# Attention scores as bf16 products over 72 rows of exact three-part splits, brought from device memory, with masks on the outer thirds and keys folded in 32-column products

## The chip, the cores and the metric

The kernel runs on one core of a Trainium2 chip. The metric is the device time of one execution in microseconds, median of the runs shown; lower is better.

## What is computed

Sliding-window attention without projections over 4096 tokens of 128 features (16 heads of 8), then a post-norm feed-forward layer, then a product-key expert layer. The part that the change touches most:

```python
H = 16; W = 32                       # heads, block of queries; keys: own block and a block on each side
kc = kp[:, :, idx, :]                # 96 keys for every 32 queries
scores = jnp.einsum('bhcqd,bhckd->bhcqk', qc, kc)
valid = (jnp.abs(rel) <= w) & (k_pos >= 0) & (k_pos < S)
scores = jnp.where(valid[None, None], scores, -1e9)
p = jax.nn.softmax(scores, axis=-1)
out = jnp.einsum('bhcqk,bhckd->bhcqd', p, vc)
```

In the expert layer, queries `x @ w_q` are normalised over all tokens and compared with keys. The kernel folds normalisation and keys into one matrix, `w_sim`, and a row of constants, `c_rows`.

## The kernel before, in words

The program has three long stages: attention (32 tiles of 128 tokens), layer norms and feed-forward (8 groups of 512 tokens), and the expert layer (32 tiles). Each engine has its own instruction list, written out by hand, and semaphores join them. In `over_pairs` a loop body is written for the first step, looped, and written for the last; in the attention stage a step is a pair of tiles.

At the start, TensorE transposes all of x into `xT` in fp32, and ScalarE copies it out of PSUM. For a tile t of the attention stage, in two halves of 8 heads each:

- GpSimd makes `queries` (the tile of `xT` times a 0/1 column for each head of a group, L457) and copies v into `v_ones` (L462); VectorE makes `windows` (`group_windows`, L1026): keys masked by group. With these zeros a product over all 128 rows gives one head's scores.
- TensorE's `scores` puts the mask into PSUM with a bf16 product over all 384 columns of a bank (L635), and adds 32 fp32 products of 96 columns (L640). Each half has two PSUM banks of its own, free again once `shift` has read them.
- VectorE's `shift` takes the row maximum (L999) and subtracts it (L1002); ScalarE's `exps` follows (L864); TensorE transposes the probabilities (L653); ScalarE copies them (L848); TensorE's `values` multiplies with v (L666); VectorE's `normalise` scales (L1011, L1015); TensorE's `attn_out` brings heads into columns (L677); VectorE's `residual` adds x from `x_tile` (L1021).

All DMAs are issued by SyncE (SP), in order. In the attention loop it loads `v_raw` for a tile when the v of two tiles before has been copied, then `x_tile` when the residual of two tiles before is done:

```python
need(sp, r1_done, t - 1)
sp.dma_start(x_tile[p][:], x[tok(t), :]).then_inc(x_in[p], 16)
```

`r1_done` counts residuals, so `x_load` of tile t waits for the residual of tile t-2. VectorE runs the residual of tile t-1 in its step t, behind a shift of tile t+1. The weights are loaded behind the first pair's loads.

After the second stage, `q_moments` to `scale_keys` on VectorE and the products L777 (constants) and L781 (16 keys, weights of 128 columns) on TensorE make `c_rows` and `w_sim`; the first similarity product (L791) of the expert stage waits for both.

## Time and profile before

| | us |
|---|---|
| median of 3 runs | 789.24 (786.45 to 789.26) |
| profiled execution, its time | 785.28 |
| profiled execution, its span | 783.4 |
| TensorE matmul busy | 624.2 (80%) |
| VectorE busy | 617.0 (79%) |
| GpSimd busy | 435.2 (56%) |
| ScalarE busy | 334.5 (43%) |
| DMA queue q1 | 37.86 MB, 19.1% of 16 engines |

The span runs from the first to the last instruction; the execution's own time holds 1.9 us more. Busy shares are means over three stages with different limits, so a stage's own rows say more than they do. The mean granted clock of TensorE is 0.933 of full speed.

### The profile page before, as it was taken

Reading aid. Unit: us, or ns where it says so; the run is one execution under the profiler, and the core shown is the slowest. Engines: PE = TensorE matmul, PEld = TensorE weight load, DVE = VectorE, ACT = ScalarE, POOL = GpSimd, SP = SyncE. Lnnn points to the kernel's source line nnn. Section 1 sums busy time; section 2 is a strip of 40 time slices with the busy share of each in tenths; the row PEclk is TensorE's granted clock in tenths of the full one; section 3 lists DMA queues with packets and bytes.
Section 4 is the critical chain, followed back from the end, with each engine's and each line's share of the span. In section 5 each row is a group of like instructions: output and inputs, shape, how many; then the busy total and the mean of one; then the engine's idle time right before and its main releaser. Section 6 shows DMA issues by size and latency. Waiting matters only on the chain.

```text
span 783.4 us, 46593 instructions
## 1 busy us (share of the span) xinstructions
PE 624.2 (80%) x19753; PEld 517.8 (66%) x19783; DVE 617.0 (79%) x1903; ACT 334.5 (43%) x514; POOL 435.2 (56%) x672
## 2 busy tenths in 40 slices
PE   5889989999988977877847487787877777777775
PEld 4667768778876855554645376676766666666674
DVE  3656747776766757999965888899999999999982
ACT  3434534545444452433320434455555455455540
POOL 4222422333232423554521778879888888898881
PEclk9999999999999998988975789999999999999997
DMA  6511111111111110000000122312222222222221
GB/s 171 196 32 38 30 29 30 37 33 35 33 36 28 34 54 14 15 28 13 0 8 3 40 62 64 70 41 67 67 67 67 64 64 67 67 67 51 58 61 41
DMA packets 45361, 38.81 MB, mean 50 GB/s; under 512 B 6512, under 2 KB 40432, under 8 KB 45040
## 3 DMA queue, kind: packets, MB, share of 16 engines
q1 hardware_dynamic: 45296, 37.86, 19.1%
q8 instruction: 51, 0.84, 0.4%
q14 instruction: 14, 0.11, 0.0%
HBM read 16.86 MB, written 2.10 MB: 24 GB/s over the span
## 4 chain that ended last, share of the span: by engine, by line
PE 41%; DVE 39%; issue 16%; POOL 1%; DVEq 1%; ACT 1%; DMA 1%; another core or an unknown queue 1%; SPq 0%; POOLq 0%; ACTq 0%
PE ps L640 12%; PE ps L653 8%; DVE top L1226 5%; PE ps L666 5%; DVE wq_sb L1257 4%; DVE prod L1281 3%; PE ps L635 3%; PE ps L806 3%; PE ps L827 3%; DVE hidT L1272 3%; DVE best L1237 2%; DVE stats L1040 2%; DVE x L1057 2%; DVE r_x L1266 2%; DVE r L1057 2%
## 5 line engine op out<-in xcount | busy, mean ns | idle before, releaser
L999 DVE TENSOR_REDUCE row_max<-ps 128x8 f32<-128x768 f32 x64 | 61.3, 958 | 77.2 <-PE ps L640 77.2
L827 PE MATMUL ps<-up_sb,prod 128*128 128x128 f32 x512 | 81.4, 322 | 46.7 <-DVE prod L1281 46.3
L462 POOL COPY v_ones<-v_raw 96x512 f32<-96x512 f32 x32 | 19.5, 609 | 168.5 <-DMA v_raw<-in_x_wrapped 168.5
L827 PEld LDWEIGHTS ps<-up_sb,prod 128*128 128x128 f32 x512 | 75.0, 229 | 53.4 <-DVE prod L1281 53.2
L864 ACT ACTIVATE arena<-arena 128x768 f32<-128x768 f32 x64 | 54.0, 844 | 125.9 <-DVE arena L1002 125.9
L640 PE MATMUL ps<-early 128*32 128x96 f32 x4096 | 102.4, 250 | 6.3 <-issue 6.3
L640 PEld LDWEIGHTS ps<-early 128*32 128x32 f32 x4096 | 86.8, 111 | 29.1 <-issue 29.1
L806 PE MATMUL ps<-arena,hidT 128*32 128x32 f32 x8192 | 82.0, 200 | 25.5 <-issue 20.8
L806 PEld LDWEIGHTS ps<-arena,hidT 128*32 128x32 f32 x8192 | 76.9, 112 | 31.0 <-issue 22.2
L557 POOL TENSOR_TENSOR wq_sb<-wq_sb,rel_exp 128x1024 f32<-128x1024 f32 x32 | 76.2, 2380 | 8.2 <-POOL rel_exp L553 7.2
L653 PE MATMUL ps<-ident,arena 128*96 128x128 f32 x512 | 70.0, 280 | 12.9 <-issue 7.6
L848 ACT ACTIVATE arena<-ps 96x512 f32<-96x512 f32 x128 | 68.6, 585 | 26.1 <-PE ps L653 26.1
L815 PEld LDWEIGHTS ps<-xT,downT_sb 128*128 128x128 f32 x512 | 63.4, 195 | 12.1 <-issue 11.1
L653 PEld LDWEIGHTS ps<-ident,arena 128*96 128x96 f32 x512 | 52.8, 127 | 24.2 <-issue 13.8
L950 ACT ACTIVATE out_tile<-ps,shift,rstd 128x128 f32<-128x128 f32 x32 | 14.7, 458 | 120.0 <-POOL shift L581 120.0
L1002 DVE TENSOR_TENSOR arena<-ps,row_max 128x768 f32<-128x768 f32 x64 | 61.3, 957 | 5.1 <-DVE row_max L999 0.2
L815 PE MATMUL ps<-xT,downT_sb 128*128 (+1 forms) x512 | 63.3, 277 | 1.5
L571 POOL TENSOR_TENSOR wqT_sb<-wqT_sb,rel_exp 128x768 f32<-128x768 f32 x32 | 63.9, 1997 | 0.4 <-issue 0.2
L1226 DVE MAX8 top<-ps 128x8 f32<-128x32 f32 x512 | 52.5, 174 | 10.2 <-remote 7.5
L457 POOL TENSOR_SCALAR early<-own_x,head_in_group 128x128 f32<-128x128 f32 x128 | 56.8, 463 | 6.6 <-POOL own_x L452 6.5
L473 POOL TENSOR_TENSOR rstd<-var_eps,minus_half 128x4 f32<-128x4 f32 (+1 forms) x18 | 22.0, 1224 | 63.6 <-DVE var_eps L1051 50.2
L666 PE MATMUL ps<-v_ones,arena 96*32 96x9 f32 x4096 | 48.4, 179 | 5.0 <-issue 5.0
(138 smaller groups left out, 1275.4 us busy)
## 6 DMA issues: line engine op xcount, KB each, us to landing
arena<-r_x SPq DMA_DIRECT2D x128, 128.0 KB, 2.4
v_raw<-in_x_wrapped SPq DMA_DIRECT2D x128, 48.0 KB, 1.8
arena<-in_x SPq DMA_DIRECT2D x8, 256.0 KB, 5.1
x_tile<-in_x SPq DMA_DIRECT2D x32, 64.0 KB, 1.8
x<-in_x SPq DMA_DIRECT2D x8, 256.0 KB, 2.8
xT_tile<-xT SPq DMA_DIRECT2D x32, 64.0 KB, 1.9
out<-out_tile SPq DMA_DIRECT2D x32, 64.0 KB, 1.5
wq_sb<-in_w_q SPq DMA_DIRECT2D x1, 1024.0 KB, 9.6
```

Source lines behind the costliest of these rows:

```text
L557: nc.gpsimd.tensor_tensor(right[p], right[p], bcast(ey.rearrange("p h j -> p j h"), 3, TERMS), ALU.mult).then_inc(right_ready, 1)
L571: nc.gpsimd.tensor_tensor(left[p][:, :, :, 0:TERMS - 1], left[p][:, :, :, 0:TERMS - 1], bcast(ex, 3, TERMS - 1), ALU.mult).then_inc(left_r ...
L640: mm = nc.tensor.matmul(ps[32 * h:32 * h + 32, g, b * WIN:(b + 1) * WIN], queries[p][:, b, h], windows[p][:, g, b * W:b * W + WIN], start= ...
L653: mm = nc.tensor.transpose(ps[0:WIN, 4 + g % 2, b * P:(b + 1) * P], probs[p][:, g * BLOCKS + b, :], ident[:])
L666: mm = nc.tensor.matmul(ps[32 * h:32 * h + 32, 6 + half, k * VW:(k + 1) * VW], probsT[g][:, b, 32 * h:32 * h + 32], v_ones[p][:, b, 4 * g ...
L806: mm = nc.tensor.matmul(slots[32 * g:32 * g + 32, k, c], leftT[p][:, r // 2, r % 2, :], blocks_of[p][:, :, r // 2, r % 2, GROUP * g:GROUP ...
L815: mm = nc.tensor.matmul(ps[:, 4 + half, (c % 4) * P:(c % 4 + 1) * P], downT_sb[:, c * P:(c + 1) * P], xT[:, tok(t)].rearrange("p (q r k) - ...
L827: mm = nc.tensor.matmul(ps[:, 6 + p, 0:P], pairs[:, c // 2, c % 2], up_sb[:, c, :], start=False, stop=(c == EC - 1))
L848: return nc.scalar.activation(out_ap, in_ap, ACT.Copy)
L999: V.tensor_reduce(mx.rearrange("p (a b) -> p a b", a=2), sc, AX_X, ALU.max).then_inc(max_done, 1)
L1002: V.tensor_tensor(shifted[p][:, at:at + 8, :].rearrange("p (a b) c -> p a b c", a=2), sc, bcast(mx.rearrange("p (a b) -> p a b", a=2), 3, ...
L1226: last = V.max(top[p][:, k, :], ps[:, p, k * KEYS:(k + 1) * KEYS])
```

## The change

x comes in transposed from the host (`xT_wrapped`), in five chunks of columns. ScalarE and VectorE split each value into three bf16 parts whose sum is exact (`split_x`), and SP writes the parts to a buffer in device memory, `terms`, laid out by pair of tiles, part, feature, head and column. For each pair of tiles SP then brings two operands of 72 partitions (8 features, 9 combinations of parts) by 5120 bf16 values, `q_rows` and `k_rows`, 10,240 bytes a partition, 737 KB each. They have two buffers: one in `early` and `xT`, one in `hid` and `prod`. A head's scores are one bf16 product over 72 rows. The mask products follow the scores and cover only the outer two thirds of each window. `queries`, `windows` and the fp32 transposes are gone; v is loaded by one DMA instead of four. TensorE's list is written by group of four tiles, with both halves of the next tile's scores ahead of where they stood; VectorE runs both shifts ahead of the rest of its step. In the folding, each key product is cut into four of 32 columns, `c_rows` is made in two parts, and ScalarE copies `w_sim`.

```diff
+    T = xT_wrapped.shape[1]
+    ROWS = 9 * DH
+    KEY_COLS = 2 * P + 2 * W
+    PART = HEADS * KEY_COLS
+    CHUNKS = ((0, 1), (1, 4), (4, 8), (8, 12), (12, 16))
...
+        terms = nc.dram_tensor("terms", (PAIRS, 5 * DH, PART), BF16, kind="Internal").ap()
...
-        windows = [early[:, p * EXPERTS:p * EXPERTS + GROUPS * (P + 2 * W)].rearrange("p (g j) -> p g j", g=GROUPS)
-                   for p in range(2)]
-        queries = [early[:, 2 * EXPERTS + p * FF:2 * EXPERTS + (p + 1) * FF].rearrange("p (b h i) -> p b h i", b=BLOCKS, h=4)
-                   for p in range(2)]
+        prod_flat = sb("prod", [P, PART // 2])
+        hid_flat = sb("hid", [P, PART // 2])
+        q_flat, k_flat = ([flat[:, 0:PART // 2].bitcast(BF16)[0:ROWS] for flat in flats]
+                          for flats in ((early, hid_flat), (xT, prod_flat)))
+        q_rows, k_rows = ([flat.rearrange("p (h t) -> p h t", h=HEADS) for flat in flats] for flats in (q_flat, k_flat))
...
+            for c in range(5):
+                sp.dma_start(x_f32[c], xT_wrapped[:, COLS[c]]).then_inc(x_f32_in[c], 16)
...
-            def b1_loads(i, first, last):
-                for p in range(2):
-                    t = 2 * i + p
-                    need(sp, v_ready, t - 1)
-                    for b in range(BLOCKS):
-                        sp.dma_start(v_raw[p][:, b, :], x_wrapped[bass.ds(t * P + b * W, WIN), :]).then_inc(v_in[p], 16)
-                    need(sp, r1_done, t - 1)
-                    sp.dma_start(x_tile[p][:], x[tok(t), :]).then_inc(x_in[p], 16)
+            def keep_terms(c):
+                sp.wait_ge(x_split, c + 1)
+                for i in range(*CHUNKS[c]):
+                    src = x_terms[c][:, :, 2 * P * (i - CHUNKS[c][0]):2 * P * (i - CHUNKS[c][0]) + KEY_COLS]
+                    for at, n in ((0, 3), (3, 2)):
+                        dst = terms[i, DH * at:DH * (at + n)].rearrange("(a c) (h t) -> (c h) a t", a=n, t=KEY_COLS)
+                        sp.dma_start(dst, src[:, 0:n]).then_inc(terms_out[c], 16)
+            def rows(i, u, landed, heads=slice(0, HEADS)):
+                part = slice(heads.start * KEY_COLS, heads.stop * KEY_COLS)
+                at = terms[bass.ds(i, 1), 0:1, part]
+                for dst, step in ((q_flat[u], 0), (k_flat[u], DH * PART)):
+                    sp.dma_start(dst[:, part], bass.AP(at.tensor, at.offset, [[PART, 3 * DH], [step, 3],
+                                                                              [1, part.stop - part.start]])
+                                 ).then_inc(landed, 16)
+            def v_load(t, p):
+                need(sp, v_ready, t - 1)
+                at = x_wrapped[bass.ds(t * P, WIN), :]
+                sp.dma_start(v_raw[p][:], bass.AP(at.tensor, at.offset, [[P, WIN], [W * P, BLOCKS], [1, P]])
+                             ).then_inc(v_in[p], 16)
+            def x_load(t, p):
+                need(sp, r1_done, t - 1)
+                sp.dma_start(x_tile[p][:], x[tok(t), :]).then_inc(x_in[p], 16)
+            def b1_loads(j, first, last):
                 if first:
+                    for p in range(2):
+                        v_load(p, p)
+                        x_load(p, p)
+                    keep_terms(0)
+                    sp.wait_ge(terms_out[0], 32)
+                    for half in range(2):
+                        rows(0, 0, first_rows_in[half], slice(8 * half, 8 * half + 8))
+                    keep_terms(1)
+                    sp.wait_ge(terms_out[1], 96)
+                    rows(1, 1, rows_in[1])
+                    for p in range(2):
+                        v_load(2 + p, p)
+                    for c in range(2, 5):
+                        keep_terms(c)
+                    for c in range(2, 5):
+                        sp.wait_ge(terms_out[c], 128)
                     load_weights()
-            over_pairs(sp, PAIRS, b1_loads)
+                    for p in range(2):
+                        x_load(2 + p, p)
+                    return
+                for u in range(2):
+                    i = 2 * j + u
+                    sp.wait_ge(scores_done, 2 * GROUPS * (i - 1))
+                    rows(i, u, rows_in[u])
+                    for p in range(2):
+                        v_load(2 * i + p, p)
+                        x_load(2 * i + p, p)
+            over_pairs(sp, NQ, b1_loads)
...
             def b1_operands(i, first, last):
                 for p in range(2):
                     t = 2 * i + p
-                    need(pool, scores_done, GROUPS * (t - 1))
-                    hold(pool)
-                    nc.gpsimd.tensor_copy(own_x[p][:], xT[:, bass.ds(t * P + W, P)]).then_inc(operands_ready, 1)
-                    pool.wait_ge(operands_ready, 5 * t + 1)
-                    hold(pool)
-                    own = own_x[p][:].rearrange("p (b j) -> p b j", b=BLOCKS)
-                    for h in range(4):
-                        nc.gpsimd.tensor_scalar(queries[p][:, :, h, :], own, head_in_group[:, h:h + 1], 1.0,
-                                                ALU.mult, ALU.mult).then_inc(operands_ready, 1)
-                    need(pool, v_in[p], 16 * BLOCKS * (i + 1))
+                    pool.wait_ge(v_in[p], 16 * (i + 1))
                     need(pool, pv_done, GROUPS * (t - 1))
...
-            def scores(t, p, half, mask_at):
+            def scores(t, j, k, half):
                 groups = (2 * half, 2 * half + 1)
-                if half == 0:
-                    pe.wait_ge(operands_ready, 5 * (t + 1))
-                    pe.wait_ge(windows_ready, t + 1)
-                    if isinstance(t, int) and t == 0:
-                        pe.wait_ge(a_copied, NQ)
+                p, u = k % 2, k // 2
+                kind = j % 2 if k == 0 else 1 + j % 2 if k == 3 else 1
+                mask_at = bass.ds(kind * (BLOCKS * WIN), BLOCKS * WIN)
+                if isinstance(t, int) and t == 0:
+                    pe.wait_ge(first_rows_in[half], 32)
+                elif half == 0:
+                    need(pe, rows_in[u], 32 * (j + u))
                 need(pe, shift_done, 2 * (t - 1) + half + 1)
-                for g in groups:
-                    nc.tensor.matmul(ps[:, g, 0:BLOCKS * WIN], ident_bf[:], mask[:, mask_at], start=True, stop=False,
-                                     skip_group_check=True)
                 for b in range(BLOCKS):
                     for g in groups:
                         for h in range(4):
-                            mm = nc.tensor.matmul(ps[32 * h:32 * h + 32, g, b * WIN:(b + 1) * WIN], queries[p][:, b, h],
-                                                  windows[p][:, g, b * W:b * W + WIN], start=False, stop=True,
+                            mm = nc.tensor.matmul(ps[32 * h:32 * h + 32, g, b * WIN:(b + 1) * WIN],
+                                                  q_rows[u][:, 4 * g + h, p * P + (b + 1) * W:p * P + (b + 2) * W],
+                                                  k_rows[u][:, 4 * g + h, p * P + b * W:p * P + b * W + WIN],
+                                                  start=b == 0, stop=False,
                                                   skip_group_check=True)
-                        if b == BLOCKS - 1:
-                            mm.then_inc(scores_done, 1)
+                def edges_of(columns):
+                    return columns.rearrange("p (b s c) -> p b s c", s=3, c=W)[:, :, 0:3:2]
+                for g in groups:
+                    nc.tensor.matmul(edges_of(ps[:, g, 0:BLOCKS * WIN]), ident_bf[:], edges_of(mask[:, mask_at]),
+                                     start=False, stop=True, skip_group_check=True).then_inc(scores_done, 1)
...
-            def b1_tile(t, p, r_next, first, last):
-                more = not (last and p == 1)
-                probs_transpose(t, p, 0)
-                if more:
-                    scores(t + 1, 1 - p, 0, mask_of(r_next))
-                probs_transpose(t, p, 1)
-                values(t, p, 0)
-                if not (first and p == 0):
-                    attn_out(t - 1, 1 - p, GROUPS * t + 3)
-                if more:
-                    scores(t + 1, 1 - p, 1, mask_of(r_next))
-                values(t, p, 1)
+            def b1_pe(j, first, last):
+                for k in range(4):
+                    t, p = 4 * j + k, k % 2
+                    following = (t + 1, j + k // 3, (k + 1) % 4)
+                    more = not (last and k == 3)
+                    if more:
+                        scores(*following, 0)
+                    probs_transpose(t, p, 0)
+                    if more:
+                        scores(*following, 1)
+                    probs_transpose(t, p, 1)
+                    values(t, p, 0)
+                    if not (first and k == 0):
+                        attn_out(t - 1, 1 - p, GROUPS * t + 3)
+                    values(t, p, 1)
...
                 for k in range(ks.start, ks.stop):
-                    mm = nc.tensor.matmul(ps[:, 6, k * KEYS:(k + 1) * KEYS], wqT_sb[:, k, :], keys_scaled[:, k, :],
-                                          start=True, stop=True)
+                    for g in range(4):
+                        mm = nc.tensor.matmul(ps[32 * g:32 * g + 32, 6, k * KEYS:(k + 1) * KEYS],
+                                              wqT_sb[:, k, 32 * g:32 * g + 32], keys_scaled[:, k, :],
+                                              start=True, stop=True)
             mm.then_inc(w_sim_done, 1)
-            pe.wait_ge(c_step, 5)
+            pe.wait_ge(c_step, 10)
...
+            for c in range(5):
+                a.wait_ge(x_f32_in[c], 16)
+                copy(x_terms[c][:, 0], x_f32[c]).then_inc(x_high, 1)
+                a.wait_ge(x_rest, c + 1)
+                copy(x_terms[c][:, 1], x_f32[c]).then_inc(x_mid, 1)
...
+            def split_x(c):
+                v.wait_ge(x_high, c + 1)
+                V.tensor_tensor(x_f32[c], x_f32[c], x_terms[c][:, 0], ALU.subtract).then_inc(x_rest, 1)
+                v.wait_ge(x_mid, c + 1)
+                V.tensor_tensor(x_terms[c][:, 2], x_f32[c], x_terms[c][:, 1], ALU.subtract).then_inc(x_split, 1)
+            split_x(0)
...
-            def group_windows(t, p):
-                need(v, scores_done, GROUPS * (t - 1))
-                V.tensor_tensor(windows[p], bcast(xT[:, tok(t, P + 2 * W)], 1, GROUPS),
-                                bcast(quadrant[:], 2, P + 2 * W), ALU.mult).then_inc(windows_ready, 1)
-            v.wait_ge(a_copied, NQ)
-            group_windows(0, 0)
-            group_windows(1, 1)
+            for c in range(1, 5):
+                split_x(c)
             shift(0, 0, 0)
...
                     if not (last and p == 1):
                         shift(t + 1, 1 - p, 0)
-                    if not last:
-                        group_windows(t + 2, p)
-                    normalise(t, p, 0)
+                        shift(t + 1, 1 - p, 1)
                     if not (first and p == 0):
                         residual(t - 1, i if p == 1 else i - 1, 1 - p)
-                    if not (last and p == 1):
-                        shift(t + 1, 1 - p, 1)
+                    normalise(t, p, 0)
                     normalise(t, p, 1)
```

TensorE (PE) in the attention loop. One tile's step before, from the start of the second tile of a pair; `early` holds queries and windows, `arena` the probabilities:

```order
L653 MATMUL ps<-ident,arena 96x128 x8
L629 ISA
L635 ISA
L635 MATMUL ps<-mask,ident_bf 128x384 x2
L640 MATMUL ps<-early 32x96 x32
L647 REGISTER_ALU
L300 REGISTER_ALU
L653 MATMUL ps<-ident,arena 96x128 x4
L300 REGISTER_ALU
L653 MATMUL ps<-ident,arena 96x128 x4
L666 MATMUL ps<-v_ones,arena 32x9 x32
L673 REGISTER_ALU
```

The same step after; `prod` and `hid` (for other pairs `xT` and `early`) are the operands that the DMAs bring. The row `L677 ISA` belongs to the mask, and the waits are not shown:

```order
L667 MATMUL ps<-prod,hid 32x96 x32
L677 ISA
L677 MATMUL ps<-mask,ident_bf 128x4x2x32 x2
L311 ISA
L687 MATMUL ps<-ident,arena 96x128 x8
L311 REGISTER_ALU
L667 MATMUL ps<-prod,hid 32x96 x32
L677 MATMUL ps<-mask,ident_bf 128x4x2x32 x2
L311 REGISTER_ALU
L687 MATMUL ps<-ident,arena 96x128 x4
L311 REGISTER_ALU
L687 MATMUL ps<-ident,arena 96x128 x4
```

The scores of the next tile's first half moved ahead of the first transposes, the second half's ahead of the second transposes and so of the values, and the mask now follows its scores.

SP in the last pair before, in the order that its loop has too (then come loads of the next stage, L376):

```order
L363 DMA v_raw<-in_x_wrapped 96x128 x4
L365 DMA x_tile<-in_x 128x128
L363 DMA v_raw<-in_x_wrapped 96x128 x4
L365 DMA x_tile<-in_x 128x128
L376 DMA x<-in_x 128x4x128 x2
```

And the last group after, again as in its loop: one pair of tiles and the next pair's operands (`scores_done` is waited for ahead of L381, `v_ready` ahead of L388, `r1_done` ahead of L393):

```order
L381 DMA early<-terms 72x1x5120
L381 DMA xT<-terms 72x1x5120
L388 DMA v_raw<-in_x_wrapped 96x4x128
L393 DMA x_tile<-in_x 128x128
L388 DMA v_raw<-in_x_wrapped 96x4x128
L393 DMA x_tile<-in_x 128x128
L381 DMA hid<-terms 72x1x5120
L381 DMA prod<-terms 72x1x5120
```

The loads of a pair's operands are new, and stand behind the `x_tile` load of the second tile of the pair before.

## Rows read from the trace of the kernel before

**Rows 1.** Chain of waits of the whole run: who waited for what, us, times, longest.

```profile
DVE row_max L999 <- PE ps L640: 77.2, 61, 4.8
```

**Rows 2.** Timeline, one tile: start us, us, engine, line, instruction, idle before it.

```profile
263.18 0.50 PE L635 MATMUL ps<-mask,ident_bf 128*128 x2
...
263.61 1.53 PE L640 MATMUL ps<-early 128*32 128x96 f32 x64
...
264.54 0.29 DVE L1021 TENSOR_TENSOR kept<-ps,x_tile 128x128 f32 x1
264.85 0.35 SPq L365 DMA_DIRECT2D x_tile<-in_x  x1
...
265.20 0.96 DVE L999 TENSOR_REDUCE row_max<-ps 128x8 f32<-128x768 f32 x1 [0.38 <-PE ps L640]
265.41 1.74 SPq L363 DMA_DIRECT2D v_raw<-in_x_wrapped  x4
...
265.76 1.07 PE L653 MATMUL ps<-ident,arena 128*96 128x128 f32 x8
266.28 0.96 DVE L1002 TENSOR_TENSOR arena<-ps,row_max 128x768 f32<-128x768 f32 x1
...
267.16 0.20 DVE L1011 RECIPROCAL rdenom<-ps 128x8 f32<-128x8 f32 x1
267.28 0.84 ACT L864 ACTIVATE arena<-arena 128x768 f32<-128x768 f32 x1 [3.10 <-DVE arena L1002]
267.39 0.22 DVE L1015 TENSOR_TENSOR heads_out<-ps,rdenom 128x64 f32<-128x64 f32 x1
...
269.71 0.72 PE L666 MATMUL ps<-v_ones,arena 96*32 96x9 f32 x64
...
270.29 0.46 PE L677 MATMUL ps<-heads_out,ident 128*32 128x32 f32 x32
270.55 0.95 DVE L1026 TENSOR_TENSOR early<-xT,quadrant 128x768 f32<-128x768 f32 x1
```

**Rows 3.** Chain that ended last, 136 to 160 us: the first transposes of two tiles.

```profile
136.32 1.07 PE ps L653 x8
...
151.77 1.08 PE ps L653 x8
```

**Rows 4.** Timeline, first shift of the stage and last value scaling.

```profile
20.34 0.96 DVE L999 TENSOR_REDUCE row_max<-ps 128x8 f32<-128x768 f32 x1 [4.79 <-PE ps L640]
...
287.60 0.22 DVE L1015 TENSOR_TENSOR heads_out<-ps,rdenom 128x64 f32<-128x64 f32 x1
```

**Rows 5.** DMA, 0 to 35 us: rate in 40 slices; issues, us to landing.

```profile
GB/s 0 0 135 346 226 222 322 323 297 291 292 226 173 125 58 86 71 73 34 26 64 301 343 390 439 412 431 407 363 395 425 390 262 99 65 24 32 0 0 0
...
up_sb<-in_up SPq DMA_DIRECT2D x1, 512.0 KB, 11.7
```

**Rows 6.** DMA of the whole page: issues with KB and us to landing.

```profile
x_tile<-in_x SPq DMA_DIRECT2D x32, 64.0 KB, 1.8
```

**Rows 7.** Timeline of the SP queue, 0 to 35 us: DMA issues.

```profile
11.39 0.43 SPq L355 DMA_DIRECT2D ln_g_all<-in_ln_g  x1
...
20.24 0.56 SPq L355 DMA_DIRECT2D up_sb<-in_up  x1
```

**Rows 8.** Windows: us, busy of PE, PEld, DVE, ACT, POOL, PEclk, DMA share, GB/s.

```profile
15.00:20.00 5.00, 3.07 (x62) 2.47 (x66) 0.55 (x1) 0.00 (x0) 4.59 (x11) 0.66 0.51 135
```

**Rows 9.** Timeline of PE after its first wait.

```profile
16.93 0.80 PE L635 MATMUL ps<-mask,ident_bf 128*128 128x384 bf16 x2 [3.97 <-POOL early L457]
17.66 2.60 PE L640 MATMUL ps<-early 128*32 128x96 f32 x64
```

**Rows 10.** Timeline of the key folding, and 32-column products later.

```profile
415.61 3.89 PE L781 MATMUL ps<-keys_scaled,wqT_sb 128*128 128x32 f32 x18
...
425.09 2.05 PE L791 MATMUL ps<-w_sim,xT_tile 128*128 128x512 f32 x2 [1.87 <-DVE c_rows L1215]
...
469.43 2.08 PE L806 MATMUL ps<-arena,hidT 128*32 128x32 f32 x217
```

133 lines of the change are left out of this document (49 added, 84 removed).

## Prediction

> **What bounds the kernel now.** I read the chain of waits first. In the attention stage VectorE's row maximum waits for the score products, 77.2 us in 61 waits [rows 1], and it is TensorE that is busy. The timeline of one tile gives each piece of its work [rows 2]: two halves of scores at 1.53 us, two masks at 0.50 (tails overlap, about 0.43), two times 8 transposes at 1.07, two times values at 0.72 (0.62 in the chain), and 0.46 for attn_out. That makes 7.6 us. A pair of tiles without gaps takes 15.45 us in the chain that ended last [rows 3]; first shift to last scaling are 20.3 and 287.8 us, 267.5 us for 32 tiles [rows 4]. VectorE's share of a tile is 4 x 0.96 (shift), 0.95 (windows), 2 x 0.42 (scale), 0.29 (residual), 5.9 us [rows 2]. So TensorE sets the pace, and faster scores would let VectorE, then 5.0 plus gaps, set it at about 5.4 us a tile. The question is whether the new operands arrive at that pace.
>
> **When a pair's operands are ordered.** In SP's list the two loads of a pair stand behind the `x_tile` load of the second tile of the pair before. For pair 3, tiles 6 and 7, that load belongs to tile 5 and waits for the residual of tile 3, which VectorE runs in its step 4, behind both shifts of tile 5. By then every score of pair 2 is done. After that residual TensorE has only the values of one half (0.7 us) before it wants tile 6's scores. So each pair's loading is almost wholly exposed: nothing covers it, though the buffer was free a pair earlier.
>
> **What a load takes.** In the trace `x_tile` is issued 0.02 us after its residual and the next DMA 0.56 us later [rows 2]. A 64 KB load lands 1.8 us after issue [rows 6]. The pair's two operands are 1.47 MB. No row shows a load of 72 partitions. Loads to 128 partitions peaked at 439 GB/s in the weights and ran near 297 with 512-byte rows [rows 5]. Bounds for the movement: 1.47/0.439 = 3.4 us if 72 partitions take no less than 128, and 1.47 over 297 x 72/128 = 167 GB/s, 8.8 us. I take the weights' rate per partition, since rows of 10 KB resemble those: 439 x 72/128 = 247 GB/s, 6.0 us. Residual to landing is then 0.6 + 1.8 + 6.0 less 0.2 counted twice, 8.2 us (5.6 to 11.0).
>
> The rows leave open whether fewer partitions cost rate. The Trainium skill, SBUF — State Buffer, section "Door 1: The DMA port swizzle", says that partitions 0 to 63 reach only 8 of 16 ports at 27.2 GB/s. By it, 1.31 MB through 218 GB/s take 6.0 us, against 3.4 by the rate in the trace; a pair would be 2.6 us apart, the kernel 36. No run here shows it yet, and it speaks against this layout.
>
> **From landing to the next order.** A half's scores are 768 columns as the mask's are, 0.50 us with its tail [rows 2]; below, 0.33 by columns, above, the 1.53 of now. I take 0.45, nearer to the bf16 row, and 0.35 for the smaller masks: 0.8 a half. Then VectorE is the path: 0.1 + 0.8 + 0.1, shifts of tile 6 at 3.9, residual 0.3, scaling 0.9 (TensorE's next scores are ready 0.2 after it), shifts of tile 7 at 3.9, 0.3 for gaps, residual 0.3: 10.6 us. Transposes, ScalarE's copies and values lie under this.
>
> **The clock.** After TensorE's idle 3.97 us at the start, a mask pair took 0.80 and a half of scores 2.60 us [rows 9], and the window's granted clock is 0.66, a mix of 1.2 and 2.4 GHz [rows 8]. With about 8 us idle in each pair I expect 1.2 GHz after each landing: first scores +0.5, transposes +0.6, second scores +0.5, less slack of 0.3: 1.3 us (0 to 2.5).
>
> Pair period: 8.2 + 10.6 + 1.3 = 20.1 us, where it was about 16.
>
> **The start.** Five chunks are split in turn: subtract, copy, subtract. By 0.96 and 0.84 us for 768 columns [rows 2], 832 columns take 3.0 and 1088 take 3.9 us. The first chunk and the mask end near 8.6 us, so the first shift starts at 8.6 + 3.0 + 3 x 3.9 = 23.3 us (it was 20.34). That is not the worst. SP loads x (2.3 MB), writes chunk 0 (landing near 11 us), loads pair 0 (to 19), writes chunk 1 (1.2 MB, to 23.5), loads pair 1 (to 31.8), writes 12 pairs of parts (4.9 MB at 297 GB/s, 16.5 us, to 48), waits for them, and only then issues the weights. Before, these took from the issue at 11.39 to the landing at 20.24 + 11.7 = 31.9: 20.5 us [rows 5, 7]. Pair 2 queues behind them: 48 + 20.5 + 6.0 = 74.5 us, where TensorE wants it near 43. One stall of some 31 us.
>
> **Ends.** Pair 15 lands at 74.5 + 13 x 20.1 = 335.8. From there to the last scaling: 10.3 + 1.3 for its shifts, 2.5 of layer-norm statistics that stand there already (read in the same timeline), 4.2 for the last exp, transposes, copies and values: 18.3, so 354.1 us instead of 287.8. +66.3.
>
> **The folding.** 64 products of 32 columns as 128 records at 2.08 us for 217 [rows 10] take 1.2 us, 2.5 at the lower clock, where 18 of now 32 take 3.89. The first similarity product started at 425.09 behind the constants; made in parts they end near 420.8. -4 (0 to -5). The DMAs of v (one for four) and GpSimd's lost work are worth nothing: both stood behind TensorE and now stand behind the loads; uncovered, v costs its 1.8 us.
>
> **Sum.** 785.3 + 66.3 - 4 = 847.6 us for a profiled execution; the median of before lies 3.9 above its profile, so 851; I say 850. In short, time = 586.3 + 13 x period, plus 3.9.
>
> **Rivals.**
> - The loads run at the full 439 GB/s and the clock stays up: period 5.6 + 10.6 + 0 = 16.2, pair 2 at 71.9: 798; with the clock's 1.3 at 815. For it: no row shows a loss with 72 partitions. Against: each partition would have to take 1.8 times what it did in the weights. 0.17.
> - The loads run at 167 GB/s, or the clock stays at 1.2 GHz: period 22.9, 891 us. Against: short rows explain the 297. 0.10.
> - Faster: the loads are ordered ahead of need, as the two buffers allow. This would need SP to pass the `r1_done` wait before the pair's last scores, 8.2 us ahead, which a residual ending earlier by a tile would give. Then a tile takes 5.6 us: 28 x 5.6 + 74.5 + 7 = 238, -50 - 4, 735 us. It decides at a period of 15.3. Against it stands the order of SP's list and of VectorE's. 0.05.
> - The bf16 products gain nothing, each half still 1.53: the first of each tile is on the path, +2.2 a pair, 880. Against: half the records and no extra passes over columns. 0.04.
> - No change: period 15.3 by a residual mix, 0.02.
>
> The forecast's own case, period 18.7 to 21.5, has 0.62, and 832 to 872 us. Range for 8 in 10: 812 to 888, from the fast-load case with the clock's price to the slow-load one. A measurement of this kernel tells changes over about 0.5%; faster by more than that 0.05, within it 0.02, slower 0.93.
>
> **What would show it.** Right: in the chain of waits TensorE's scores (L667) wait for the operands' DMA, 13 to 15 times some 7 to 8 us; an issue of 737 KB lands 6 to 8.5 us after it; issued only after the residual of L1047; first shift near 23 us, last weights near 68, pair 2 near 74; last scaling near 354; granted clock in the stage well below 0.98; half a tile's scores 0.4 to 0.6 us; folding shorter by 4. Wrong: operands landing before the pair's shifts end, waits under 3 us, or tiles at 6 us. If terms or weights move faster than I price, the one stall shrinks, by at most 20 us.

## The result, and the profile of the changed kernel

The changed kernel takes 966.5 us (median of 5 runs, 964.1 to 971.9), the kernel before 786.5 (5 runs, 782.9 to 789.3) in the same comparison. The ratio is 1.229, with a 95% interval of 1.225 to 1.233. It is slower, as predicted, but by 180 us and not by 64: the forecast was 850, and the range ended at 888. The profiled execution of the changed kernel took 971.9 us, with a span of 970.0.

The page of the changed kernel. The line PEclk is TensorE's granted clock in 40 slices of 24 us, in tenths of full speed, q8 is the queue that brings instructions (packets, MB, share of the DMA engines), and after it comes the chain that ended last:

```profile
span 970.0 us, 42022 instructions
PE 591.0 (61%) x17799; PEld 489.0 (50%) x17799; DVE 598.4 (62%) x1884; ACT 339.8 (35%) x517; POOL 370.5 (38%) x510
...
PEclk9776765767567676776899986799799999999987
...
q8 instruction: 95, 1.56, 0.7%
...
DVE 30%; PE 29%; DMA 16%; issue 16%; SPq 6%; POOL 1%; DVEq 1%; ACT 0%; POOLq 0%; ACTq 0%
DMA xT<-terms 8%; DMA prod<-terms 7%; PE ps L687 6%; PE ps L849 5%; DVE top L1247 4%; PE ps L667 3%; PE ps L828 3%; DVE prod L1302 3%; PE ps L700 3%; SPq L374 3%; DVE wq_sb L1278 2%; PE ps L677 2%; SPq L381 2%; DVE best L1258 2%; DVE stats L1059 2%
```

The DMA of the rows and "issue", time in which an engine waited for nothing that the profile shows, hold 16% of the chain each. The waits of TensorE from 90 to 450 us say which they are (the place, what it waited for, us in total, times, longest):

```profile
PE ps L667 <- DMA prod<-terms: 72.1, 7, 11.2
PE ps L667 <- DMA xT<-terms: 55.7, 6, 9.6
PE ps L700 <- issue: 38.6, 25, 2.4
PE ps L667 <- issue: 18.3, 5, 3.8
```

The first two are the exposed loads of the prediction, 13 times 9.8 us. The last two, 57 us, are in no sentence of it. L700 are the products of the values, in the middle of which nothing is waited for. Where [rows 1] had VectorE waiting for TensorE's products 77.2 us in 61 waits, it now waits 225.3 us in 51.

The timeline of one pair (start, duration, engine, line, what; in brackets the idle time before it and its cause):

```profile
179.44 0.28 DVE L1047 TENSOR_TENSOR kept<-ps,x_tile 128x128 f32 x1
...
179.75 0.34 SPq L393 DMA_DIRECT2D x_tile<-in_x  x1
...
180.75 0.81 SPq L381 DMA_DIRECT2D early<-terms  x1
181.77 0.82 SPq L381 DMA_DIRECT2D xT<-terms  x1
...
181.85 0.44 PE L700 MATMUL ps<-v_ones,arena 96*32 96x9 f32 x17 [2.39 <-issue]
...
182.92 0.35 SPq L388 DMA_DIRECT2D v_raw<-in_x_wrapped  x1
...
191.71 0.83 PE L667 MATMUL ps<-xT,early 72*32 72x96 bf16 x32 [9.42 <-DMA xT<-terms]
...
193.12 0.96 DVE L1025 TENSOR_REDUCE row_max<-ps 128x8 f32<-128x768 f32 x1 [10.33 <-PE ps L677]
...
198.78 0.66 PE L700 MATMUL ps<-v_ones,arena 96*32 96x9 f32 x53
199.21 0.29 DVE L1047 TENSOR_TENSOR kept<-ps,x_tile 128x128 f32 x1 [1.14 <-PE ps L711]
...
201.31 0.30 PE L700 MATMUL ps<-v_ones,arena 96*32 96x9 f32 x11 [1.88 <-issue]
...
205.38 0.83 PE L667 MATMUL ps<-xT,early 72*32 72x96 bf16 x32 [3.78 <-issue]
```

Two things are to be seen. The chain residual, `x_tile`, rows, landing, scores runs as it was argued: residual to 179.72, rows issued from 180.75, scores at 191.71, 12.0 us. And the group of 64 products that began at 198.78 stops after 53, waits 1.88 us and goes on with 11; 3.78 us later the next scores start, whose rows have been there since 191.7. The second break is the jump back of TensorE's loop, the first lies 11 products ahead of it. In both an instruction packet is on its way: one from 198.9 to 200.1, one from 202.4 to 203.7. The break at the jump comes in nearly every turn (the last row of the waits has five).

Stretches of the changed kernel (busy us of PE, PEld, DVE, ACT and POOL with instructions; granted clock, share of the DMA engines, GB/s):

```profile
90.00:450.00 360.00, 175.06 (x6344) 145.57 (x6343) 125.69 (x235) 97.86 (x156) 15.88 (x26) 0.68 0.29 75
```

TensorE works less than half of the stretch. A granted clock of 0.68 is a mix of the two levels, 1.2 and 2.4 GHz, with more of the lower; in the kernel before, the stage had 0.99.

### The profile page after: what moved, and what is told of

It reads as the page before. It is cut to its first block, busy times and chain, and to the rows that moved or that the text cites. A ratio compares the mean times of both kernels' runs of the same rounds, so it can differ in the third digit from the quotient of the medians.

```text
span 970.0 us, 42022 instructions
## 1 busy us (share of the span) xinstructions
PE 591.0 (61%) x17799; PEld 489.0 (50%) x17799; DVE 598.4 (62%) x1884; ACT 339.8 (35%) x517; POOL 370.5 (38%) x510
## 4 chain that ended last, share of the span: by engine, by line
DVE 30%; PE 29%; DMA 16%; issue 16%; SPq 6%; POOL 1%; DVEq 1%; ACT 0%; POOLq 0%; ACTq 0%
DMA xT<-terms 8%; DMA prod<-terms 7%; PE ps L687 6%; PE ps L849 5%; DVE top L1247 4%; PE ps L667 3%; PE ps L828 3%; DVE prod L1302 3%; PE ps L700 3%; SPq L374 3%; DVE wq_sb L1278 2%; PE ps L677 2%; SPq L381 2%; DVE best L1258 2%; DVE stats L1059 2%
## 5 line engine op out<-in xcount | busy, mean ns | idle before, releaser
L1025 DVE TENSOR_REDUCE row_max<-ps 128x8 f32<-128x768 f32 x64 | 61.2, 956 | 225.3 <-PE ps L677 225.3
L828 PE MATMUL ps<-arena,hid 128*32 128x32 f32 x8192 | 82.3, 200 | 26.5 <-issue 22.9
L667 PE MATMUL ps<-xT,early 72*32 72x96 bf16 x1024 | 24.6, 264 | 120.1 <-DMA xT<-terms 101.7
L687 PE MATMUL ps<-ident,arena 128*96 128x128 f32 x512 | 94.8, 348 | 0.3 <-ACT arena L870 0.3
L828 PEld LDWEIGHTS ps<-arena,hid 128*32 128x32 f32 x8192 | 77.3, 112 | 31.9 <-issue 24.2
L687 PEld LDWEIGHTS ps<-ident,arena 128*96 128x96 f32 x512 | 81.2, 167 | 7.4 <-issue 1.9
L667 PEld LDWEIGHTS ps<-xT,early 72*32 72x32 bf16 x1024 | 18.4, 127 | 127.4 <-issue 94.8
L700 PE MATMUL ps<-v_ones,arena 96*32 96x9 f32 x4096 | 54.8, 181 | 44.1 <-issue 44.0
L700 PEld LDWEIGHTS ps<-v_ones,arena 96*32 96x32 f32 x4096 | 47.0, 113 | 54.0 <-issue 53.9
L667 PE MATMUL ps<-prod,hid 72*32 72x96 bf16 x1024 | 22.1, 244 | 82.5 <-DMA prod<-terms 80.9
L837 PEld LDWEIGHTS ps<-xT,downT_sb 128*128 128x128 f32 x512 | 64.1, 197 | 12.2 <-issue 11.3
L667 PEld LDWEIGHTS ps<-prod,hid 72*32 72x32 bf16 x1024 | 16.3, 116 | 87.8 <-issue 69.5
```

The lines of the kernel that those rows point to most:

```text
L667: mm = nc.tensor.matmul(ps[32 * h:32 * h + 32, g, b * WIN:(b + 1) * WIN], q_rows[u][:, 4 * g + h, p * P + (b + 1) * W:p * P + (b + 2) * W] ...
L687: mm = nc.tensor.transpose(ps[0:WIN, 4 + g % 2, b * P:(b + 1) * P], probs[p][:, g * BLOCKS + b, :], ident[:])
L700: mm = nc.tensor.matmul(ps[32 * h:32 * h + 32, 6 + half, k * VW:(k + 1) * VW], probsT[g][:, b, 32 * h:32 * h + 32], v_ones[p][:, b, 4 * g ...
L828: mm = nc.tensor.matmul(slots[32 * g:32 * g + 32, k, c], leftT[p][:, r // 2, r % 2, :], blocks_of[p][:, :, r // 2, r % 2, GROUP * g:GROUP ...
L837: mm = nc.tensor.matmul(ps[:, 4 + half, (c % 4) * P:(c % 4 + 1) * P], downT_sb[:, c * P:(c + 1) * P], xT[:, tok(t)].rearrange("p (q r k) - ...
L1025: V.tensor_reduce(mx.rearrange("p (a b) -> p a b", a=2), sc, AX_X, ALU.max).then_inc(max_done, 1)
```

## The experiments

Medians; the kernel before took 786.7, 787.9, 788.6 and 790.9 us in the four groups (1 to 4, 5 to 8, 9 to 11, 12). The theories: *loads* (the waits for the rows are exposed and longer than priced) and *body* (TensorE's loop body of four tiles, twice the old one, is not held and is brought again in each turn). Their rivals stand in the expectations.

**1. The loads by themselves.** A kernel that only orders row loads one after the other; it computes nothing of the layer.

```diff
+                for dst, s in tests:
+                    sp.dma_start(dst, s).then_inc(done[n], 16)
+                    sp.wait_ge(done[n], 16)
...
+                sp.dma_start(q72_step0[0:72], q).then_inc(done[n], 16)
+                sp.dma_start(k72_step8[0:72], k).then_inc(done[n + 1], 16)
+                sp.wait_ge(done[n], 16)
+                sp.wait_ge(done[n + 1], 16)
```

> This kernel computes nothing; it loads rows of 10,240 bytes from x, each DMA waited for before the next: 72 rows in the pattern of the q operand (24 rows, each three times), 72 in that of the k operand, 72 plain, 64 plain on partitions 0 to 63, 64 on partitions 32 to 95, 96, 128, and 128 rows of 5,760 bytes (as many bytes as 72 of 10,240), twice; then q and k back to back, and the short 128-row form back to back. In the changed kernel the pair took 10.8 us from first issue to landing, 1.47 MB. Theory of partitions: all three 72-row forms take the same, near 5.5 us, the 128-row form of the same bytes near 3.7, and 64 rows on 32 to 95 are at least 1 us faster than on 0 to 63. Rival, source: the q pattern, which reads each row three times, is slower than 72 plain rows by over 1 us. Rival, company: all are fast here (q and k together under 8 us) and only the company of other traffic in the kernel makes 10.8.

The DMA issues (KB each, us from issue to landing), then the SP queue:

```profile
plain<-in_x SPq DMA_DIRECT2D x2, 1280.0 KB, 5.4
plain<-in_x SPq DMA_DIRECT2D x3, 720.0 KB, 6.1
short<-in_x SPq DMA_DIRECT2D x3, 720.0 KB, 4.2
...
plain<-in_x SPq DMA_DIRECT2D x2, 640.0 KB, 5.2
upper<-in_x SPq DMA_DIRECT2D x2, 640.0 KB, 4.4
```

```profile
89.25 0.85 SPq L55 DMA_DIRECT2D q_step<-in_x  x1
90.14 0.81 SPq L56 DMA_DIRECT2D k_step<-in_x  x1
99.10 0.78 SPq L55 DMA_DIRECT2D q_step<-in_x  x1
```

128 rows of 10 KB take 5.4 us, 72 rows with little over half the bytes take 6.1, and the same bytes over 128 partitions 4.2: fewer partitions do cost rate, and each form is 0.5 to 0.6 us slower than the theory had it (5.5 and 3.7). 64 rows on partitions 32 to 95 (`upper`) are 0.8 us faster than on 0 to 63, not 1. The ordering of the source (each row read three times) costs little: the next issue followed 6.4 to 6.6 us after q or k. The two operands together take 9.85 us, and 10.1 the second time, from the first issue until both have landed and the next is issued. So most of the 10.8 us from issue to landing in the kernel are the loads' own, where 1.8 + 6.0 less 0.2 had been priced, and other traffic adds about 1.

**2. Loads ordered ahead.** The rows of pair i + 1 are ordered in the place of pair i.

```diff
-                    sp.wait_ge(scores_done, 2 * GROUPS * (i - 1))
-                    rows(i, u, rows_in[u])
...
+                        sp.wait_ge(scores_done, 2 * GROUPS * i)
+                        rows(i + 1, 1 - u, rows_in[1 - u])
```

> The changed kernel with one shift in SP's list: in the place where it ordered pair i's operands it orders those of pair i+1, a whole pair earlier; the start is as it was. Theory of order: the waits of the score products for DMA vanish after pair 2 (12 of them, 9 to 12 us each), and the kernel falls by 100 to 150 us, to 815 to 865. Rival, rate: the loads themselves or their traffic bound the stage, waits of 5 us or more stay and the kernel stays above 900.

870.9 us, ratio 1.111 (1.103 to 1.118): just above the range of the order theory, 815 to 865, and below the rival's 900. The waits for the rows are gone, and others have come (TensorE, 90 to 450 us; then two rows of its timeline):

```profile
PE ps L703 <- issue: 85.1, 30, 7.4
PE ps L670 <- issue: 20.1, 6, 3.8
```

```profile
119.90 0.83 SPq L381 DMA_DIRECT2D hid<-terms  x1
120.84 0.79 SPq L381 DMA_DIRECT2D prod<-terms  x1
...
131.00 0.39 PE L703 MATMUL ps<-v_ones,arena 96*32 96x9 f32 x11 [7.27 <-issue]
```

The break in the group of value products is 7.3 us where rows are on their way, ordered at 119.90, and was 1.9 in the changed kernel after they had landed. The same place in the six turns of the loop has 1.9 to 2.0 us each time in the changed kernel, and 7.3, 7.0, 6.1, 7.0, 4.0 and 2.3 here. The trace shows which part grew. The packet of instructions takes about 1.2 us in either run (128.37 to 129.53 here, 198.87 to 200.06 there), but here it starts 4.6 us after TensorE stopped, and there 0.6 us before. Between 123.7 and 128.3 us the row loads and other data keep the DMA engines 84% busy. The wait moved from the operands to the instructions; that the packet stands behind the rows is the likely reason, and not tried apart.

**3 and 4. No row loads, with four and with two tiles in the body.** From pair 2 on the scores read the rows of pairs 0 and 1 (in run 4 of pair 0 alone): the loads of the loop are left out.

```diff
-                    sp.wait_ge(scores_done, 2 * GROUPS * (i - 1))
-                    rows(i, u, rows_in[u])
```

Run 4 besides has two tiles a turn in place of four:

```diff
-            over_pairs(pe, NQ, b1_pe)
+            over_pairs(pe, PAIRS, b1_pe)
...
```

> The changed kernel without the operand loads of pairs 2 to 15: all score products read the buffers of pairs 0 and 1, so the scores of later tiles are not the reference's. It gives the stage's pace free of loads. If nothing but the loads slowed the stage, a tile takes 5.6 us and the kernel about 735. If TensorE's instruction supply (idle put down to issue: 1.3 to 3.8 us in three of four tiles, 9 us in each loop body of four) is a cost of its own, a tile takes 7 to 8 us and the kernel about 790.

> The same with TensorE's loop body of two tiles instead of four, all scores from the buffer of pair 0 (again not the reference's scores). Theory of the long body: the issue gaps come from fetching a body of four tiles at each turn and shrink to at most 1 us a tile, 20 to 60 us less than the four-tile body. Rival: the gaps follow the number of instructions passed, not the body's length, and both bodies take the same within 10 us.

One run each: 813.1 us, where 735 or about 790 was expected, and 725.0 us. Both do the same products without any load of rows in the loop. The length of the body is worth 88 us, more than the 20 to 60 expected, with what the clock lost by the breaks in it (granted 0.87 over the whole of run 3, 0.91 of run 4). The row of the instruction queue tells them apart (packets, MB, share): of run 3, then of run 4.

```profile
q8 instruction: 95, 1.56, 0.8%
```

```profile
q8 instruction: 38, 0.62, 0.4%
```

With the body held, that is, not brought again, residuals follow each other by 5.4 and 4.7 us (149.95, 155.31, 160.05): what bf16 products would give, were their operands free.

**5. TensorE's stage written out.** No loop turn is left; loads and order as changed.

```diff
-            over_pairs(pe, NQ, b1_pe)
+            for j in range(NQ):
+                b1_pe(j, j == 0, j == NQ - 1)
```

> The changed kernel with one edit: TensorE's attention stage is written out for its 32 tiles, so that its instructions come in a straight line and no block of them is fetched twice for a loop turn; loads, masks and every other engine stay as changed. If the four-tile loop body of TensorE costs what the pair of runs without loads showed (813.1 with four tiles a turn against 725.0 with two, 88 us), the idle stretches that end on issue before the score products vanish, a pair takes about 22 us where it took 27.6, and the time comes to 870 to 900. If those gaps belong to something else (the row loads, the clock, a wait that the profile does not show), or if a straight line is fetched no better than a turn, it stays at 950 to 970. The exposed row loads stay in either case, at 11 to 12 us from the residual of a pair to its scores.

933.2 us, ratio 1.184 (1.176 to 1.191): 33 us won, half or less of what was expected, and 31 us in 20 breaks on issue are left. A straight line is fetched once, but its 32 tiles are as many as the loop's turns bring, each turn anew: 88 packets instead of 95. So little less comes in, and that while the rows move. The body theory was right in direction and wrong in this size.

**6. The kernel before with a body of four tiles.**

```diff
...
-            with pe.Fori(1, BP) as j:
-                b1_tile(2 * j, 0, 2 * j + 1, False, False)
-                b1_tile(2 * j + 1, 1, (2 * j + 2) % TB, False, False)
...
+            with pe.Fori(1, NQ - 1) as j:
+                for k in range(4):
+                    b1_tile(4 * j + k, k % 2, (4 * j + k + 1) % TB, False, False)
...
```

> The kernel before, float32 scores and no loads of rows, with one edit: TensorE's attention loop has four tiles in its body, as the changed kernel has, where it had two. If a body of four tiles is by itself too long to be held, the same work takes 6 to 12 us more in each of the 6 turns of the loop: 825 to 865 against about 787, with idle stretches on issue in TensorE once or twice a turn and more packets on the queue of instructions (about 95 against 51). If the gaps of the changed kernel came from its row loads or from the clock and not from the body, it stays within 4 us of the kernel before.

850.0 us, ratio 1.080 (1.073 to 1.086). Nothing but TensorE's attention loop differs, and it costs 62 us without a row load in sight. The rows of this run, then those of the kernel before:

```profile
q8 instruction: 111, 1.82, 0.9%
...
L640 PE MATMUL ps<-early 128*32 128x96 f32 x4096 | 114.3, 256 | 24.6 <-issue 24.6
L640 PEld LDWEIGHTS ps<-early 128*32 128x32 f32 x4096 | 92.4, 114 | 54.6 <-issue 54.6
```

```profile
q8 instruction: 51, 0.84, 0.4%
...
L640 PE MATMUL ps<-early 128*32 128x96 f32 x4096 | 102.4, 250 | 6.3 <-issue 6.3
```

This run has 111 packets, where the kernel before has 51, and TensorE's idle time on issue ahead of the scores is 24.6 us instead of 6.3. It is the cleanest run of the study: the body theory holds, and row loads beside the fetches are not needed for it.

**7. Both taken away, and the start mended.** Stage written out, rows of q and k of the next pair at two places with v ahead of them, pair 2 ahead of the last chunks and weights.

```diff
+                    v_load(2 * i, 0)
...
+                        sp.wait_ge(scores_done, 2 * GROUPS * i)
+                        rows(i + 1, 1 - u, rows_in[1 - u], both=(0,))
+                    x_load(2 * i, 0)
+                    v_load(2 * i + 1, 1)
...
+                        rows(i + 1, 1 - u, rows_in[1 - u], both=(1,))
+                    x_load(2 * i + 1, 1)
```

> The changed kernel with both costs taken away and the start mended: TensorE's attention stage written out for its 32 tiles; the rows of pair i+1 ordered a pair ahead, queries and keys in two places of the queue with the rows of v ahead of them; and the rows of pair 2 and the tiles x of pair 1 ordered ahead of the last two chunks of terms and of the weights. If exposed loads and the loop body together were the loss, a pair takes 10.5 to 14 us and the time is 700 to 770, under the kernel before. If the loads are bound by the bandwidth of the queue (9.9 us a pair when they run alone, beside v_raw and x_tile), a pair takes 15 to 18 us and the time is 780 to 840. If neither was the cause, 860 or more, as with the loads ordered ahead alone (870.9).

843.9 us, ratio 1.068 (1.060 to 1.077): just above the range of the bandwidth rival. A pair takes 19.0 us (rows issued at 138.4 and, 8 pairs later, at 290.0), and in 120 to 240 us TensorE waits on issue alone, 33 us. Neither the theory's 10.5 to 14 us a pair nor the rival's 15 to 18 came. The breaks that are left are of the kind that run 2 showed of the loop; as there, that the fetches stand behind the row loads is likely and not shown. The start was not mended either: once, at 92.3 us, the values waited 20.2 us for v, whose load was issued at 80.1, behind the weights.

**8. The folding alone, on the kernel before.**

```diff
+                    for g in range(4):
+                        mm = nc.tensor.matmul(ps[32 * g:32 * g + 32, 6, k * KEYS:(k + 1) * KEYS],
+                                              wqT_sb[:, k, 32 * g:32 * g + 32], keys_scaled[:, k, :],
...
+                split_constants(part)
```

> The kernel before with the folding stage of the change alone: key products of 32 columns, constants split in two parts, w_sim copied by ScalarE. The prediction put it at -4 us, from 10.6 us between the keys and the first similarity: 782 to 784 against 786 to 787. Rival: the stage gives its time back in the first tiles of the expert stage, whose starts wait for something else, and the time stays within 1 us of the kernel before.

786.3 us (12 runs), ratio 0.997 (0.994 to 1.000): 1.6 us less by the medians, with an interval from nothing to 5 us, between the theory and its rival. In the profile the stage is 4 us shorter, as forecast: from the first constants product to the first similarity product it takes 6.6 us. In the kernel before it takes 10.6, from the first row here to the 425.09 of [rows 10]; the other rows are of this run:

```profile
414.49 1.33 PE L777 MATMUL ps<-keys_shifted,ones 128*128 128x288 f32 x2 [5.01 <-DVE keys_shifted L1191]
```

```profile
420.31 1.33 PE L777 MATMUL ps<-keys_shifted,ones 128*128 128x288 f32 x2 [5.00 <-DVE keys_shifted L1195]
...
421.57 1.19 PE L782 MATMUL ps<-keys_scaled,wqT_sb 128*32 128x32 f32 x72
...
426.89 2.08 PE L793 MATMUL ps<-w_sim,xT_tile 128*128 128x512 f32 x2 [2.18 <-DVE c_rows L1221]
```

**9. All loads, in their order, with a body of two tiles.** Both tiles of a turn can name one pair of buffers only, so each pair is loaded into the same two.

```diff
-                          for flats in ((early, hid_flat), (xT, prod_flat)))
+                          for flats in ((early, early), (xT, xT)))
...
-            over_pairs(pe, NQ, b1_pe)
+            over_pairs(pe, PAIRS, b1_pe)
```

> The changed kernel with a TensorE body of two tiles and all loads kept, whole and in the same places of the queue. The two tiles of a turn can name one pair of buffers only, so every pair is loaded into the same two; that should add no wait, since the order of the queue issues the rows of a pair behind the residual of three tiles back, later than the last scores of the pair before. If the four-tile body costs what its removal saved without loads (88 us), the stretches on issue vanish, a pair takes about 21 to 22 us where it took 27.6, and the time is 870 to 890. If company of the row loads made the gaps and not the body, or if the single buffer adds a wait of its own, it is 940 or more.

920.7 us, ratio 1.167 (1.161 to 1.173): 46 us won, not 77 to 97. The waits of TensorE, 90 to 450 us:

```profile
PE ps L666 <- DMA xT<-terms: 151.5, 13, 11.9
PE ps L666 <- issue: 3.3, 13, 0.3
PE ps L699 <- issue: 3.1, 2, 1.6
```

The breaks are nearly gone (9 us in all, from 57), and 38 packets are left of 95. But the wait for rows rose from 9.8 to 11.7 us: TensorE now reaches it earlier, so part of what the breaks cost had been time that it would have waited anyway. A pair takes 24.0 us (rows issued at 100.9 and, 8 pairs later, at 293.1).

**10. The same with the rows ordered first,** directly behind the last scores of the pair before.

```diff
+                    x_load(2 * i, 0)
+                    v_load(2 * i + 1, 1)
...
+                        sp.wait_ge(scores_done, 2 * GROUPS * (i + 1))
+                        rows(i + 1, 0, rows_in[0])
+                    x_load(2 * i + 1, 1)
```

> The run with two tiles a body, and the rows of the next pair ordered directly behind the last scores of the pair in the buffers, ahead of the wait for the residual; the rows of pair 2 and the tiles x of pair 1 go ahead of the last chunks of terms and the weights. The order of the queue then costs nothing, the single buffer leaves the load of 11 to 12 us open, less the work of about 5 us that is left of the tile in flight: a pair is 11.5 + 5.5 = 17 us, 4 to 5 less than with the order kept, and the start loses its 25 to 30 us stall: 790 to 830. If the load takes as long as it is given (bound by bandwidth in company), it stays at 860 or more.

872.3 us, ratio 1.107 (1.101 to 1.112): not the 790 to 830 of the theory, but in the range of its rival, a load that takes as long as it is given. A pair takes 20.8 us (rows issued at 113.2 and, 8 pairs later, at 279.9), and 8.1 of them are the wait for the rows: 3.2 us a pair won by order alone, where 17 us a pair had been expected. The load itself did not get shorter: from the issue at 153.90 to the scores at 164.99 are 11.1 us. Of the stall at the start less was won than expected, since the next wait there was for v: its load, issued at 83.8 behind the weights, held the values of tile 4 for 17.8 us (L704).

**11. A quarter of the rows.** From pair 2 on only the rows of 4 of 16 heads are loaded; the other scores are of older rows.

```diff
-                    rows(i, u, rows_in[u])
+                    rows(i, u, rows_in[u], slice(0, 4))
```

> The changed kernel, four-tile body and order kept, with loads from pair 2 on that bring only the rows of the first 4 of 16 heads (the scores of the other heads are of older rows): 180 KB instead of 720 KB a buffer, the same two issues. By the size theory the time from issue to landing falls from 10.8 to 3.5 to 4.5 us, 14 pairs win about 6.5 each and the time is 870 to 885, with the stretches on issue left. If the wait is mostly fixed (issue, first byte, the write of the semaphore) or the gaps of TensorE cover it, less than 30 us are won: 935 to 966.

885.1 us, ratio 1.123 (1.117 to 1.128): 81 us won, at the upper edge of the size theory's range. The 13 waits for rows fall from 127.8 to 50.3 us, 3.9 each. From first issue to scores are 5.1 us (181.36 to 186.48) instead of 11.0, for a quarter of the bytes: most of the load goes with its size, and part of it does not. The breaks on issue stay, 62 us.

**12. The folding and the masks on the outer thirds, on the kernel before.**

```diff
-                    nc.tensor.matmul(ps[:, g, 0:BLOCKS * WIN], ident_bf[:], mask[:, mask_at], start=True, stop=False,
...
+                    nc.tensor.matmul(edges_of(ps[:, g, 0:BLOCKS * WIN]), ident_bf[:], edges_of(mask[:, mask_at]),
+                                     start=False, stop=True, skip_group_check=True).then_inc(scores_done, 1)
...
```

> The kernel before with two parts of the change that need no terms and no loads: the mask products over the outer thirds only, placed behind the score products of their half, and the folding stage. A mask pair took 0.50 us before and takes 0.39 in the changed kernel at the same clock, twice a tile: 32 tiles x 2 x 0.11 = 7 us less work on TensorE, if TensorE's work sets the pace of a tile, and with 1 to 2 us of the folding 777 to 781 against 787. Rival: behind the scores the mask lies on the way to the row maximum, where ahead of them it lay beside a wait, which gives back 0.39 us a half where TensorE had waited: 785 to 800.

780.5 us against 790.9, ratio 0.989 (0.984 to 0.993), in the theory's range of 777 to 781. Of the versions that compute the layer it is the only one clearly faster than the kernel before. One mask product takes 278 ns where it took 326. The mask products of this run in the attention stage and who waited for them (us, times), then those of the kernel before:

```profile
L645 PE MATMUL ps<-mask,ident_bf x66: 272/278/283, 150.1 to 277.3; 128*128 x62, 128*128 128x256 bf16 x4
...
  DVE row_max L1005: 29.6, 23
```

```profile
L635 PE MATMUL ps<-mask,ident_bf x64: 326/326/337, 152.7 to 279.4; 128*128 x60, 128*128 128x384 bf16 x4
```

The row maximum now waits for the mask, but the price that the rival named does not show in it: from 150 to 277 us of the kernel before it waited 32.4 us, in 31 waits, for the scores. The profiled run gives 3 us in the attention stage and 4 in the folding, and 2 are given back in the rest. What is left of the 10 is no difference between the profiles: that of the kernel before was, at 785.3, one of its fastest.

## Why the prediction was right in sign and wrong in size

**Right: what bounds and what the order does.** The stage waits for rows that are ordered behind the residual of three tiles back, 13 times in 90 to 450 us, and its first shift starts at 22.2 us (forecast 23.3). The bf16 scores of half a tile take 0.52 us at the upper clock and 0.83 at the lower (forecast 0.45). The folding stage became 4.0 us shorter, as forecast, though alone it moved the median by only 1.6 (run 8). A slip without effect: the pieces of one tile of the kernel before add up to 7.8 us and not 7.6, which is nearer to the 15.45 of a pair.

**The accounts.** The last value scaling ends at 467.9 us, 180.1 later than in [rows 4]; +66.3 was forecast. The missing 114 us are 11 at the start (scores of pair 2 at 85.63 instead of 74.5), 98 in the period (pair 15 comes 359.8 us later, at 445.39: 13 times 27.67 us instead of 20.1) and 4 in the tail. Behind the stage, -4 of folding stand against +4 in the middle stage and +7 in the expert stage of the profiled run, the slowest of five.

**The step that failed: a pair's period as the sum of load, shifts and clock.** It had three terms, and a fourth was missing.

- Missing: TensorE's loop body. The prediction followed SP's, VectorE's and TensorE's order and never asked what the new loop, four tiles in place of two, does to TensorE's own instructions. Run 9 gives it 3.6 us a pair (27.67 to 24.03) and 46 us in all; where no load wait covers the fetches they cost more, 62 us in the kernel before (run 6) and 88 without loads (runs 3 and 4). How long the code is can be estimated from the instruction queue: run 5 has 26 tiles more in its text than run 9 and 0.82 MB more on q8 (1.44 and 0.62), 31.5 KB a tile, so a body of four is 126 KB. By its records (308 matmuls a tile for 244), a tile of the kernel before is about 40 KB, its body of two 80 KB and that of run 6 about 159. Bodies of 63 and 80 KB were held, those of 126 and 159 were not. The count of packets fits this: with every turn of four tiles brought anew, as many tiles come in as in run 5's straight line, and 95 packets are near its 88.
- Too small: the load. Residual to landing was put at 8.2 us, with 11.0 as the upper bound, and measured 12.0 and 11.3 in the two kinds of pair. 72 rows run slower than the rate of the weights per partition says: the two loads alone take 9.85 to 10.1 us instead of 7.6 (run 1), other traffic adds about 1, and 1.0 instead of 0.6 lies ahead of the first issue; run 11 shows that the bytes make most of it. Over both kinds of pair that is 3.4 us.
- About right: from landing to the next residual 11.9 us, with the clock; run 9, which has hardly any breaks, has 12.3 (208.44 to 220.69). The rest, 0.5 us.

3.6, 3.4 and 0.5 make the 7.57 (27.67 less 20.1), but for rounding.

**The start.** The SP queue of the changed kernel:

```profile
46.42 5.19 SPq L374 DMA_DIRECT2D terms<-last_terms  x8
56.02 0.36 SPq L365 DMA_DIRECT2D ln_g_all<-in_ln_g  x1
...
66.07 0.56 SPq L365 DMA_DIRECT2D up_sb<-in_up  x1
66.67 0.91 SPq L393 DMA_DIRECT2D x_tile<-in_x  x2
68.00 0.83 SPq L381 DMA_DIRECT2D early<-terms  x1
```

The weights were issued from 56.0 us, where the terms had been priced to be out by 48: 8 of the 11 us are the terms'. The rows of pair 2, issued at 68.0, came with the weights, and their scores start at 85.6: 29.6 us after the first weight's issue, where 26.5 had been priced. Run 10 ordered them earlier, and another load came late in their place.

**The rivals.** Loads at 167 GB/s (891 us) was the nearest, right in the size of the load and without the body. "Faster, by loads ordered ahead" gave 735: order alone (run 2) came to 871, with 105 us of breaks on issue in place of the waits for rows. Run 4's 725 shows that the arithmetic of that rival was fair, had the code been held and the rows been there.

The Trainium skill, Runtime: NRT & Kernel Launch, section "Instruction fetch mechanics", says that TensorE holds 128 KiB of instructions, refilled in blocks of 16 KiB, and that a taken branch whose target is outside the current window of two pages stalls for a fetch. Runs 6 and 9 agree that a jump back to code that is not held costs time; of the size they show something else. Bodies of 63 and 80 KB, longer than two such blocks, were held, and one of about 126 KB, just under 128 KiB, was not. The page also says that crossing a block in a straight line is mostly hidden. Run 5 differs, with 31 us of breaks in 90 to 450 us beside the row loads, and the measurement decides. By the port rule of the Trainium skill (SBUF — State Buffer, "Door 1: The DMA port swizzle") the prediction put the two loads 2.6 us apart. Run 1 agrees in direction and shows 3.3 to 3.5: 9.85 and 10.1 us for 72 rows, and 6.6 for two loads of the same bytes over 128 partitions (109.19 to the next issue at 115.78).

**Still open.** Why a fetch starts so late while row loads are on their way (breaks of up to 7.3 us against 1.9) is read from two traces, not tried apart; a version with the rows on another queue, or with fewer instructions for the same products, would tell. What two buffers, a body of two tiles and loads ordered ahead would give together was not tried. Where between 80 and 126 KB a body stops being held was not measured.

## What to carry to other kernels

When a change makes a loop body longer, count its instructions in bytes before counting its work: the row of the instruction queue on the page tells at a glance whether the body is held (38 packets or 95), and breaks on "issue" inside a group of like products tell where it isn't. Before counting on a load ordered ahead, see what else is fetched in that time: here the waits for rows turned into longer waits for instructions (run 2). And price loads to part of the partitions by a run of their own; a rate from loads to all of them, scaled, made 7.6 us of 9.85.

## What the runs showed of the hardware

- A loop body of TensorE of 63 or 80 KB, by the estimate above, was held (38 and 51 packets in all), one of 126 or 159 KB was brought again in every turn (95 and 111). Run 9 had 57 packets of 16.4 KB less than the changed kernel and took 46 us less; run 4 had as many less than run 3 and took 88 us less.
- The break at one fetch grew from 1.9 to 7.3 us with 1.47 MB of rows on their way; the packet took about 1.2 us in both cases and started 4.6 us after TensorE stopped instead of 0.6 us before (run 2 and the changed kernel).
- Rows of 720 KB in all land in 6.1 us on 72 partitions and in 4.2 on 128; 64 rows of 10 KB take 5.2 us on partitions 0 to 63 and 4.4 on 32 to 95 (run 1).
- TensorE was idle about 10 us in each pair of tiles, and its clock was at the lower level, 1.2 GHz, after that wait: granted 0.68 over 90 to 450 us, transposes of half a tile at 1.92 us after the wait and 1.04 later in the pair.
